# Stacked bf16 rows for two cross-attentions: spread by transfers through memory, not by spread copies and transposes

## The reference, cut to what matters

```python
x = x + _L0_xattn_ref(ctx_1024, ctx_1024, _layernorm(x), w_out, b_out)   # keys, values = ctx, queries = normalised x
x = x + _L0_ffn_ref(_layernorm(x), ...)                                  # 8 experts, top 2, 128 -> 512 -> 128
x = x + _L1_xattn_ref(_layernorm(x), ctx_1024, ctx_1024, Wq, bq, Wk, bk, Wv, bv, Wo, bo)   # with projections
x = x + _L1_ffn_ref(...)
...
scores = q @ k.T * scale        # per batch (2) and head (16): 256 x 512, 8 terms per product
out = softmax(scores) @ v
```

## Time and profile before

| | us |
|---|---|
| median of 3 runs | 650.02 |
| lowest and highest | 649.97, 653.85 |
| the profiled execution's own time | 649.92 |
| its span, first to last instruction | 648.1 |
| PE, DVE, ACT, POOL busy | 523.1, 401.3, 323.6, 99.5 |
| mean granted clock | 0.894 |

### The profile page before, as it was taken

The page is one execution under the profiler, slowest core; times in us unless marked ns, Lnnn a source line. Parts: engine busy times, 40 slices in busy tenths (PEclk is TensorE's granted clock), DMA queues, the critical chain, the costliest instruction groups (busy, mean ns, idle before and its releaser), DMA issues. The chain is left out here.

```text
span 648.1 us, 9553 instructions
## 1 busy us (share of the span) xinstructions
PE 523.1 (81%) x3481; PEld 309.2 (48%) x3482; DVE 401.3 (62%) x1039; ACT 323.6 (50%) x535; POOL 99.5 (15%) x102
## 2 busy tenths in 40 slices
PE   2669995799984699959788557899999647985997
PEld 2624443477774244435365222455555536553565
DVE  6888853356755988528734465877776366552544
ACT  3626782444432277823635524877777013552421
POOL 4400000000002000000616059500000040000000
PEclk9877999699995779988899777999999966997899
DMA  8900000000000200000000000000000500000000
GB/s 214 407 7 0 2 3 17 0 1 2 0 10 28 98 1 2 1 1 1 0 1 0 1 1 0 0 2 2 1 2 1 196 0 1 1 2 1 1 0 18
DMA packets 3094, 16.55 MB, mean 26 GB/s; under 512 B 348, under 2 KB 860, under 8 KB 2396
## 3 DMA queue, kind: packets, MB, share of 16 engines
q1 hardware_dynamic: 3048, 15.94, 7.2%
HBM read 15.68 MB, written 0.26 MB: 25 GB/s over the span
## 5 line engine op out<-in xcount | busy, mean ns | idle before, releaser
L495 ACT ACTIVATE PR<-ps 128x1024 f32<-128x1024 f32 x80 | 77.1, 982 | 32.0 <-PE ps L1326 16.2
L761 DVE TENSOR_REDUCE mxs<-ps 128x1 f32<-128x512 f32 x128 | 81.5, 682 | 12.6 <-PE ps L1284 11.6
L1270 PE MATMUL ps<-identb,REP 128*96 128x128 bf16 x464 | 39.2, 261 | 30.1 <-DVE REP L298 23.6
L1284 PE MATMUL ps<-Kst,Qst 96*128 96x512 bf16 x128 | 52.3, 458 | 11.2 <-DVE mxs L761 8.8
L843 DVE TENSOR_REDUCE nm<-ps 128x1 f32<-128x512 f32 x64 | 41.2, 685 | 25.5 <-PE ps L1428 25.5
L406 POOL TENSOR_SCALAR ve<-mv 128x4 f32<-128x4 f32 x11 | 2.6, 237 | 350.8 <-DVE mv L716 291.6
L1270 PEld LDWEIGHTS ps<-identb,REP 128*96 128x96 bf16 x464 | 37.6, 158 | 31.8 <-DVE REP L298 19.6
L544 ACT ACTIVATE Qst<-ps,nm 128x512 f32<-128x512 f32 x64 | 44.9, 701 | 4.1 <-DVE nm L843 4.1
L536 ACT COPY PR<-ps 128x512 f32<-128x512 f32 x64 | 37.4, 588 | 18.7 <-PE ps L1439 18.7
L1316 PE MATMUL ps<-Qst,Kst 108*128 108x256 bf16 x256 | 42.7, 293 | 0.5 <-ACT PR L495 0.5
L504 ACT COPY Qst<-ps 12x1024 bf16<-12x1024 bf16 x24 | 24.0, 1000 | 34.8 <-PE ps L1351 34.7
(11 more groups left out here) (320 smaller groups left out, 991.8 us busy)
## 6 DMA issues: line engine op xcount, KB each, us to landing
FC<-in_fc SPq DMA_DIRECT2D x2, 2048.0 KB, 18.5
FC<-in_w SPq DMA_DIRECT2D x1, 2048.0 KB, 8.7
REP<-in_w SPq DMA_DIRECT2D x1, 1536.0 KB, 6.5
FC<-in_w2e SPq DMA_DIRECT2D x1, 1024.0 KB, 10.8
rows_t<-in_rows SPq DMA_DIRECT2D x1, 909.5 KB, 10.9
wd_t<-in_w_d SPq DMA_DIRECT2D x1, 872.5 KB, 24.6
VX<-in_w SPq DMA_DIRECT2D x1, 576.0 KB, 21.6
VX<-in_b SPq DMA_DIRECT2D x1, 576.0 KB, 22.7
```

The costliest lines, as they stand in the source:

```text
L495: act.activation(PRg[:, g % 2, u * 1024:u * 1024 + width], bank(3 + 2 * (n % 2), 2)[:, 0:width], ACT.Exp, scale=scale).then_inc(s.p_ready, 1)
L761: i = dve.tensor_reduce(m[:, u // 4, u % 4:u % 4 + 1], bank(n % 2), AX_X, ALU.max)
L1270: i = pe.transpose(bankb(lot_bank(n))[0:PAD, h * P:(h + 1) * P], REPv[:, tl % 4, h0 + h, :], identb[:, :])
L1284: i = pe.matmul(bank(n % 2), Qst[0:PAD, h, q0:q0 + P], Kst[0:PAD, h, b * SK:(b + 1) * SK], start=True, stop=True)
```

## The change

The 24 tiles of the first two cross-attentions are no longer spread and transposed. Instead:

- Keys and queries are taken with their columns on the partitions (128 = 16 heads x 8). For the first keys that is `ctxT`, which is loaded anyway. The first queries come from PE's transpose of the normalised x. The second keys and queries come from projections with the operands exchanged, so that one matmul of 512 columns gives 512 tokens of all heads (`keys1`, and two for the keys in all). `split_rows` splits them into three bf16 parts in `REP` (as `Kparts` and `Qparts`).
- SP stores each part to a scratch array in memory, rearranged (`k_rows` 24x16x1024; `q_rows` 40x16x512, where two of the three parts are stored twice so that any three in a row can be read at once), and loads `Kst` and `Qst` from it, three times 24 partitions per batch (`store_keys`, `load_keys`, `store_queries`, `load_queries`). A load is issued after SP has waited for the stores.
- The rows of the maxima move to partitions 0 to 11, and the split rows to 12 to 83. Both matmuls of the scores now contract over 84 rows. GpSimd clears the maxima's rows before each of the two attentions.
- The order of SP's queue changes at the start: x, ctxT, const, sel and ctx, then all the stores and loads of the first attention, and only then `rows_t` and the other weights.
- In the expert loop the second keys take two matmuls with splits on DVE (experts 1, 2) and the second values two sets of four matmuls (experts 3, 4).

```diff
+            def store_keys(phase, b):
+                for i in range(NPART):
+                    sp.wait_ge(s.k_split, NPART * (2 * phase + b) + i + 1)
+                    sp.dma_start(Kscr[HD * i:HD * (i + 1), :, b * SK:(b + 1) * SK].rearrange("c h k -> h c k"),
+                                 Kparts[:, i, b * SK:(b + 1) * SK]).then_inc(S[f"k{phase}_stored{b}"], 16)
+            def load_keys(phase, b):
+                sp.wait_ge(S[f"k{phase}_stored{b}"], 16 * NPART)
+                for a in range(NPART):
+                    sp.dma_start(Kst[MAXR + PROWS * a:MAXR + PROWS * (a + 1), :, b * SK:(b + 1) * SK],
+                                 Kscr[:, :, b * SK:(b + 1) * SK]).then_inc(S[f"k{phase}_loaded{b}"], 16)
+            def store_queries(phase, b):
+                for i in range(NPART):
+                    sp.wait_ge(s.q_split, NPART * (2 * phase + b) + i + 1)
+                    for at in ((i, i + NPART) if i < 2 else (i,)):
+                        sp.dma_start(Qscr[HD * at:HD * (at + 1), :, b * SQ:(b + 1) * SQ].rearrange("c h k -> h c k"),
+                                     Qparts[:, i, b * SQ:(b + 1) * SQ]).then_inc(S[f"q{phase}_stored{b}"], 16)
+            def load_queries(phase, b):
+                sp.wait_ge(S[f"q{phase}_stored{b}"], 16 * (NPART + 2))
+                for a in range(NPART):
+                    sp.dma_start(Qst[MAXR + PROWS * a:MAXR + PROWS * (a + 1), :, b * SQ:(b + 1) * SQ],
+                                 Qscr[HD * a:HD * a + PROWS, :, b * SQ:(b + 1) * SQ])\
+                        .then_inc(S[f"q{phase}_loaded{b}"], 16)
...
+            def split_rows(to, src, r, bias, done):
+                def less(part):
+                    if bias is None:
+                        return dve.tensor_tensor(r, src, part, ALU.subtract)
+                    return dve.scalar_tensor_tensor(out=r, in0=src, scalar=bias, in1=part, op0=ALU.add,
+                                                    op1=ALU.subtract)
+                first = dve.tensor_copy(to[:, 0, :], src) if bias is None else \
+                    dve.tensor_scalar(to[:, 0, :], src, bias, None, ALU.add)
+                signal(first, done)
+                link(less(to[:, 0, :]))
+                signal(dve.tensor_copy(to[:, 1, :], r), done)
+                link(dve.tensor_tensor(r, r, to[:, 1, :], ALU.subtract))
+                signal(dve.tensor_copy(to[:, 2, :], r), done)
...
+            dve.wait_ge(s.ld_x, 16)
+            variances(0)
+            dve.wait_ge(s.ld_ctxT, 16)
+            split_rows(Kparts[:, :, 0:SK], ctxT[:, 0:SK], rest[:, 0:SK], None, 'k_split')
+            normalised(0)
+            split_rows(Kparts[:, :, SK:NK], ctxT[:, SK:NK], rest[:, 0:SK], None, 'k_split')
+            dve.wait_ge(s.xn_turned, 1)
             for b in range(B):
...
+                split_rows(Qparts[:, :, b * SQ:(b + 1) * SQ], bank(0)[:, b * SQ:(b + 1) * SQ], rest[:, 0:SQ], None,
+                           'q_split')
             dve.wait_ge(s.ld_rows, 16)
             add_row("bo0")
             attention(0)
...
+                if a < 2 and g in (0, G // 2) and part == 0:
+                    pe.wait_ge(S[f"k{a}_loaded{b}"], 16 * NPART)
+                    pe.wait_ge(S[f"q{a}_loaded{b}"], 16 * NPART)
...
-                        i = pe.matmul(bank(n % 2), Qst[0:PAD, h, q0:q0 + P], Kst[0:PAD, h, b * SK:(b + 1) * SK],
+                        i = pe.matmul(bank(n % 2), Qst[0:ROWS_A, h, q0:q0 + P], Kst[0:ROWS_A, h, b * SK:(b + 1) * SK],
...
-            for t in range(NT):
-                i = pe.matmul(bank(2)[:, t * P:(t + 1) * P], lnT[:, t * P:(t + 1) * P], WB["wq1"],
-                              start=True, stop=True)
-            i.then_inc(s.q2_ready, 1)
-            stack(PHASE_TILES[1][8:12])
-            stacked(pe, PHASE_TILES[1][-1])
+            pe.matmul(bank(2), WB["wq1"], lnT[:, :], start=True, stop=True).then_inc(s.q2_ready, 1)
+            pe.wait_ge(s.q_split, 2 * B * NPART)
+            pe.wait_ge(s.rows_zero, 2)
+            pe.wait_ge(s.v1_read, B)
             attention(1)
```

More of the change, by code:

```diff
@@ L46 @@
 MROW = PAD + 4 * NPART
+PROWS = NPART * HD
+MAXR = 4 * NPART
+ROWS_A = MAXR + NPART * PROWS
 VW = 32
@@ L246, in mega_kernel @@
             lots_till.append(len(lots))
[L248 to L251, removed]
+        ROPE_TILES = range(0, 8)
         def stacked(eng, till_tile):
@@ L420, in _ @@
             rstd_of(2)
-            for n in K1:
-                spread(pool, n)
+            pool.wait_ge(s.st_ready, UNIT[1])
+            clear_max_rows()
             rstd_of(3)
-            for n in PHASE_TILES[1][8:12]:
-                spread(pool, n)
             rstd_of(4)
@@ L555, in _ @@
             act.wait_ge(s.setup_dve, 1)
-            for b in range(B):
-                spread_and_stack(act, range(6 * b, 6 * b + 6), range(6 * b, 6 * b + 6))
             warm(ACT.Exp)
@@ L988, in _ @@
             normalise(3)
-            spread_and_stack(dve, [], [K1[E - 1]])
             dve.wait_ge(s.q2_ready, 1)
-            link(dve.tensor_tensor(Onat[:, :, :], bank(2).rearrange("p (t n) -> p t n", t=NT),
-                                   RB["bq1"].unsqueeze(1).to_broadcast([P, NT, P]), ALU.add))
-            split(Onat.rearrange("p t n -> p (t n)"), 0, T)
-            spread_and_stack(dve, PHASE_TILES[1][8:12], PHASE_TILES[1][8:12])
+            for b in range(B):
+                dve.wait_ge(S[f"q0_stored{b}"], 16 * (NPART + 2))
+                split_rows(Qparts[:, :, b * SQ:(b + 1) * SQ], bank(2)[:, b * SQ:(b + 1) * SQ], rest[:, 0:SQ],
+                           CB["bq1"], 'q_split')
             add_row("bo1")
@@ L1543, in _, with keys1, values1 @@
             pe.wait_ge(s.ld_ctxT, 16)
-            def keys_values(t):
-                if t >= 2:
-                    pe.wait_ge(s.stack_dve, lots_till[K1[t - 2]] // 2)
-                if t:
-                    pe.wait_ge(s.kv1_read, t)
-                pe.matmul(bank(6)[:, 0:P], ctxT[:, t * P:(t + 1) * P], WB["wk1"], start=True, stop=True)
-                pe.matmul(bank(6)[:, P:2 * P], ctxT[:, t * P:(t + 1) * P], WB["wv1"],
-                          start=True, stop=True).then_inc(s.kv1_ready, 1)
+            def keys1(b):
+                if b:
+                    pe.wait_ge(s.k_split, NPART * (B + 1))
+                pe.matmul(bank(6), WB["wk1"], ctxT[:, b * SK:(b + 1) * SK], start=True, stop=True)\
+                    .then_inc(s.k1_ready, 1)
+            def values1(b):
+                if b:
+                    pe.wait_ge(s.v1_read, b)
+                else:
+                    pe.wait_ge(s.k_split, NPART * 2 * B)
+                for k in range(4):
+                    i = pe.matmul(bank(6)[:, k * P:(k + 1) * P], ctxT[:, (4 * b + k) * P:(4 * b + k + 1) * P],
+                                  WB["wv1"], start=True, stop=True)
+                i.then_inc(s.v1_ready, 1)
             expert_up(0)
```

193 lines of the change are left out of this document (96 added, 97 removed).

## The result

The change made the kernel slower: 666.11 us median (665.13 to 667.32, four runs) against 650.0 us, a ratio of 1.0247 [1.0221, 1.0272]. The prediction, 645.7 us (638 to 657), was wrong in sign and size. The profiled execution took 665.13 us with a span of 663.2, against 649.92 and 648.1.

A forecast was written before the change was run, and what follows sets the result against it. Bounds: a chain of handovers at the start and before the second attention, PE in the expert loop. Terms -7.9 + 7.7 - 4.0 = -4.2 us from 649.92 gave 645.7 us, range 638 to 657.

The forecast's parts named there:

- the sum: Whole program: expert loop -7.9, start +7.7, stretch before the second attention -4.0, together -4.2 us.
- part 2: Start: the chain through SP's stores and loads moves the first maximum from 37.39 to 45.1 us, +7.7 us.
- part 3: Second query projection's end to the next maximum: 9.7 us, before 13.4; with a shorter matmul, -4.0 us.
- the named one: Start: DVE waits for `rows_t`, landed at 44.4 us, before its first maximum at 45.1; PE stands too.
- my own formula: Start: first maximum changes by 3456/r - 11.5 us, r being the loads' rate in KB/us, taken as 180.
- SP's issuing as the bound: Rival, groups of three loads: slow issuing delays last data, four times, +4, 650 us; inside forecast's band, no own chance.
- GpSimd's clears and casts lie before 15 us and beside the chain.: Start: GpSimd's work, its largest fill 3.5 us, was expected to add nothing to the chain.
- Attentions costed at nothing: First two cross-attentions: length unchanged, 0 us, although PE comes in idle and its clock may be low.
- if the attentions themselves change length by more than 2 us: First two cross-attentions: one of the signs named in advance that would show the forecast wrong.
- My price of a late rise: First attention groups: PE's clock rising 3.4 us later loses about 1.7 us; earlier, it gains that.
- Part 1: Expert loop, bound by PE: transposes go, 6.3 us, and waits for DVE, 1.5 us; sum -7.9 us.
- The slower rival: First attention: loads bound by few partitions, `rows_t` waiting behind them; at rate 100, +13.7, 663.6 us; chance 0.16.

## Why the prediction was wrong

**The failed steps** are two terms of the sum, part 2 and part 3, and two costs put at nothing, the attentions and GpSimd's fills. The sum said -4.2 us and the profiled executions differ by +15.2. Of these 19.4 us, 7.8 lie at the start, 6.7 in the two attentions, 3.1 between the experts and attention 1, and 1.5 ahead of the experts.

*Part 2, the start, +7.7 us: right in its mechanism, wrong in its size.* The wait was the named one, and taking it away gave back 16.8 us. Along the predicted steps: the last key store was issued at 16.0 (15.1 predicted); the first query stores had landed at 27.57 (24.2), 2.5 us more; the second at 42.90 (36.6), 2.9 more; `rows_t` was added at 52.14, 9.2 us later (7.8), 1.4 more. With 0.9 at the beginning that is 7.7 more of 7.8. The rate was not the main error: by my own formula 161 GB/s in place of 180 gives 3456/161 - 11.5 = +10.0, so 2.3 us. The 0.9 at the beginning is the held cast, less what was faster there. More than half of the remaining 4.6 us can be read in the stretches above. The query stores moved at the loads' 160 GB/s, in one stream with them, and not at the 304 of wide transfers that I gave them: 320 KB cost 0.9 us more, twice (an estimate from the two rates). And where stores handed over to loads, nothing moved for 2.2 us, twice, where my steps have 1.7 (23.5 to 25.2). The rest I haven't taken apart. SP's issuing was mispriced too (0.8 us a load and 0.62 a query store, not 0.4), but in between it didn't bind: SP had issued the first query stores by 21.73 and waited until 27.57 for them to land. So what the rival "SP's issuing as the bound" describes is not what made the start longer, as far as the trace shows; it does show in part 3 below.

*"GpSimd's clears and casts lie before 15 us and beside the chain."* They do lie there, but DVE's cast under the fill took 3.81 us and not 0.43. The transposed context had landed 2.1 us earlier than I reckoned (by 4.68, not 6.8), which hid a good part of it. A second fill did the same ahead of the experts, 3.0 us. Moving both gave 4.2.

*Attentions costed at nothing*, against +2.2 and +4.5. I had named the sign that would be wrong ("if the attentions themselves change length by more than 2 us") but sought its reason in PE's coming in idle. With 128 rows the clock rose early though PE was just as idle; what moved the rise in both attentions, both ways, is the number of rows that the score matmuls contract. I had priced PE's score matmuls by columns alone. My price of a late rise was if anything too high (1.7 us for 3.4, against a measured third of a microsecond for one); that the rise would come 7 and 12 us later was not foreseen. It cost 6.7 us, more than the whole predicted gain, and going to 128 rows gave back 7 to 9.

**Part 1** held: the loop itself, from the first expert's input to the last add, fell by 9.3 us, from 73.0 to 63.8 (7.9 predicted), and PE has no idle time in it. The stretch gained only 6.4 since the fill took 3.0 ahead of it.

**Part 3** failed in size: 12.5 us and not 9.7, 1.1 of it up to the issue of the first load, as the stores were issued one by one, and 1.6 in the loads. Splitting the issuing between two engines gave back 0.9.

**The slower rival** (rate 100, 663.6 us) gave nearly the right time for a wrong reason: the rate was 161. Its chance, 0.16, was too small because slower outcomes were tied to the rate alone, whereas here costs of other kinds, each named and put at little or nothing (handovers, issuing, the fills, the attentions' length), had the same sign.

## What to carry to other kernels

When work moves from engines to transfers, count the handovers: each costs its issue on the queue, the data already in front of it on the same DMA engines, and a pause (2.2 us here) between the last stored byte and the first loaded one; and a small load that everyone waits for must not stand last. Don't cost a fill on GpSimd or a smaller operand at nothing since "it is beside the chain" or "takes the same cycles": look at what runs at the same moment on DVE, and at when PE's clock rises. If an attention's length changes while its instructions don't, compare the stretch from its first matmul to the rise.

## What the runs showed of the hardware

- Beside a 3.6 us fill on GpSimd one DVE cast took 3.81 us instead of 0.43, and beside a 3.5 us one four scalings took 4.07 instead of 1.11; with the fills moved they took 0.42 and 1.11. The second fill was on 12 partitions and held them as the one on 128 did.
- With score matmuls over 84 rows the granted clock rose 26 to 32 us after an attention's first maximum (six profiled executions), with 108 and 128 rows after 14 to 20 (six others). In the edited kernels the added rows were all zero. What the chip looks at is not shown.
- The loads, 384 pieces each, took the issuing engine 0.8 us each, the query stores, 128 pieces, 0.62, and `rows_t` 0.54.
- Stores in ScalarE's queue, the last issued at 15.5 us, had landed only at 22.66, behind loads of SP's queue issued from 9.98.
- Between the last data of query stores and the first data of the loads that waited for them, no data moved for 2.2 us, twice.
- Loads into 24 neighbouring partitions moved at 147 GB/s in 1 KB pieces and at 146 in 16 KB ones.
- The clock's records begin only at 79.2 us in the changed kernel's trace, and before them the stretches show 1.00 although matmuls take half-level times: there the durations have to be read.
